# Cross attention in a decoder layer: the two halves of the output product in blocks (3, 0) and (3, 1) instead of (1, 6) and (1, 7)

## The reference

```python
def _L0_xattn_ref(x, context, context_mask, Wq, Wk, Wv, Wo):     # x is layer-normalised
    q = (x @ Wq).reshape(B, N, HEADS, hd).transpose(0, 2, 1, 3)   # 16 heads of 16
    k = (context @ Wk).reshape(B, M, HEADS, hd).transpose(0, 2, 1, 3)
    v = (context @ Wv).reshape(B, M, HEADS, hd).transpose(0, 2, 1, 3)
    scores = jnp.einsum('bhid,bhjd->bhij', q, k) * scale
    scores = jnp.where(context_mask[:, None, None, :], scores, max_neg)
    attn = jax.nn.softmax(scores, axis=-1)
    out = jnp.einsum('bhij,bhjd->bhid', attn, v)
    return out.transpose(0, 2, 1, 3).reshape(B, N, DIM) @ Wo      # x = x + this
```

## Time and profile before

| | |
|---|---|
| median of 3 runs | 1402.81 us (1402.61 to 1403.64) |
| the profiled execution | 1404.3 us |
| its span, first to last instruction | 1402.2 us |
| mean granted TensorE clock | 0.947 |
| PE busy | 1238.2 us, 88% of the span |
| DVE busy | 986.9 us, 70% |
| ACT busy | 629.1 us, 45% |
| POOL busy | 279.6 us, 20% |

### The profile page before, as it was taken

The page is one execution under the profiler, slowest core; times in us unless marked ns, Lnnn a source line. Parts: engine busy times, 40 slices in busy tenths (PEclk is TensorE's granted clock), DMA queues, the critical chain, the costliest instruction groups (busy, mean ns, idle before and its releaser), DMA issues. The chain is left out here.

```text
span 1402.2 us, 21352 instructions
## 1 busy us (share of the span) xinstructions
PE 1238.2 (88%) x6678; PEld 742.9 (53%) x6679; DVE 986.9 (70%) x1769; ACT 629.1 (45%) x1174; POOL 279.6 (20%) x224
## 2 busy tenths in 40 slices
PE   6699999999999996769999999899999724999976
PEld 4478777877787776413343343334333212666655
DVE  3787787778788773677778768666888166666646
ACT  4233333333333332217677757665877621433432
POOL 1322222222222221001200200120000023555540
PEclk9899999999999999759999999999999966999998
DMA  5000000000000000562810660173130070111125
GB/s 195 0 1 1 1 1 1 1 2 1 1 1 1 1 0 25 147 129 50 153 25 7 110 116 1 30 121 60 58 124 1 0 219 19 58 60 54 58 74 155
DMA packets 61367, 72.39 MB, mean 52 GB/s; under 512 B 14472, under 2 KB 52744, under 8 KB 60632
## 3 DMA queue, kind: packets, MB, share of 16 engines
q1 hardware_dynamic: 53064, 56.58, 17.3%
q0 software_dynamic: 3792, 10.36, 2.4%
q10 hardware_dynamic: 4416, 4.20, 0.9%
HBM read 52.08 MB, written 18.78 MB: 51 GB/s over the span
## 5 line engine op out<-in xcount | busy, mean ns | idle before, releaser
L1318 DVE TENSOR_REDUCE neg_max<-pS 128x1 f32<-128x1024 f32 x256 | 306.8, 1220 | 72.1 <-PE pS L1025 70.3
L1178 ACT ACTIVATE pt<-pR 128x512 f32<-128x512 f32 x512 | 287.4, 601 | 101.9 <-PE pR L1047 95.2
L1047 PE MATMUL pR<-qs,ks 100*128 100x512 bf16 (+1 forms) x512 | 188.6, 386 | 9.0 <-issue 4.2
L1025 PE MATMUL pS<-ks,qs 100*128 (+1 forms) x512 | 162.2, 401 | 11.2 <-DMA qs<-q_scr 5.7
L1059 PE MATMUL b_pO<-pt,b_v 128*32 128x512 f32 x1024 | 137.3, 608 | 3.3 <-ACT pt L1178 2.7
L1047 PEld LDWEIGHTS pR<-qs,ks 100*128 100x128 bf16 (+1 forms) x512 | 49.3, 98 | 155.2 <-issue 75.7
L232 PE MATMUL pP<-w_feat,a_xT 128*128 128x512 f32 x256 | 123.1, 606 | 2.7 <-DVE kf L488 1.5
L171 POOL TENSOR_TENSOR kf<-kf,fsum 128x2048 f32<-128x2048 f32 x16 | 57.9, 3620 | 215.6 <-DVE fsum L498 215.6
L171 POOL TENSOR_TENSOR qf<-qf,fsum 128x2048 f32<-128x2048 f32 x16 | 58.8, 3673 | 184.7 <-DVE fsum L498 184.7
L290 PE MATMUL pO<-v,am 128*128 128x96 f32 x512 | 91.2, 275 | 0.0
L406 ACT COPY qfT<-pT 128x512 f32<-128x512 f32 x64 | 37.0, 579 | 116.0 <-PE pT L258 116.0
(11 more groups left out here) (295 smaller groups left out, 2136.1 us busy)
## 6 DMA issues: line engine op xcount, KB each, us to landing
k_scr<-parts SPq DMA_DIRECT2D x24, 256.0 KB, 2.8
qs<-q_scr SPq DMA_DIRECT2D x18, 256.0 KB
ks<-k_scr SPq DMA_DIRECT2D x6, 768.0 KB
ks<-in_L_ffn_w_dram SPq DMA_DIRECT2D x2, 2048.0 KB, 9.9
ks<-in_L_ffn_w_dram SPq DMA_DIRECT2D x4, 1024.0 KB, 11.4
c_y<-y_rows SPq DMA_DIRECT2D x16, 256.0 KB, 3.2
cx<-in_ctx_dram SPq DMA_DIRECT2D x4, 768.0 KB, 9.6
q_scr<-parts SPq DMA_DIRECT2D x12, 256.0 KB, 2.6
```

Of the source, the lines that this page charges most:

```text
L1025: ins = pe.matmul(pS1[:, slot, 512 * half:512 * half + 512], qs[0:KR, bass.ds(par, 1), h, P * t:P * t + P].rearrange("r a n -> r (a n)"), ...
L1047: pe.matmul(ring[bank], ks[0:KR, bass.ds(par, 1), h, P * j:P * j + P].rearrange("r a n -> r (a n)"), qs[0:KR, bass.ds(par, 1), h, :].rearr ...
L1178: nc.scalar.activation(pt[:, j % 2, i, :], ring[bank], ACT.Exp).then_inc(exp_done, 1)
L1318: nc.vector.tensor_reduce(neg_max[:, hg % 2, u // G, u % G:u % G + 1], pS1[:, u % 2, :], AX_X, ALU.max, negate=True).then_inc(max_done, 1)
```

## The change

The plan has the steps ("y", 0) and ("y", 1) in blocks (3, 0) and (3, 1), where there was no step, instead of (1, 6) and (1, 7). By the order above, ("m_turn", 2) becomes the last and only step of (1, 6). The statistics of the last batch skip blocks (3, 0) and (3, 1), since those of batch 2's rows (the last four of the twelve) need its "y" steps done; they wait for the steps so far before the first and before the ninth tile.

```diff
-                (1, 6): [("m_turn", 2), ("y", 0)], (1, 7): [("y", 1)],
+                (1, 6): [("m_turn", 2)],
                 (2, 0): [("v", 0)], (2, 1): [("v", 1)], (2, 2): [("o_turn", 1)],
                 (2, 3): [("v", 2)], (2, 4): [("v", 3)], (2, 6): [("m_turn", 3)],
-                (3, 2): [("o_turn", 2)], (3, 6): [("m_turn", G)],
+                (3, 0): [("y", 0)], (3, 1): [("y", 1)], (3, 2): [("o_turn", 2)], (3, 6): [("m_turn", G)],
...
-                            if last and 2 <= hg and t_next < T - TB:
-
-                                if t_next == 0:
+                            if last and 2 <= hg and (hg, j) not in ((3, 0), (3, 1)) and t_next < T - TB:
+
+                                if t_next in (0, T - 2 * TB):
                                     wait(dve, emptied, start + n)
                                 nc.vector.bn_stats(stats[:, t_next, :], xr[:, t_next, :])
```

## The result

| | before | after |
|---|---|---|
| median of 6 runs | 1402.71 us (1400.61 to 1403.64) | 1394.34 us (1393.56 to 1397.29) |
| profiled execution, span | 1404.3, 1402.2 us | 1394.68, 1392.5 us |
| mean granted clock in it | 0.947 | 0.951 |

The ratio of the runs is 0.995, 95% interval 0.9937 to 0.9963: 7.0 us less, between 5.2 and 8.8. The two medians of the table differ by 8.4. The forecast was 1394.3 and 8.5 less. So the kernel is faster, by the two ratios a little less than forecast, though 8.5 lies inside both intervals. The median itself came out to the tenth, and part of that is luck, as the further profiles of the kernel before show.

What follows compares the result with a forecast made beforehand. PE was taken to bound cross attention. The terms -12.6 - 4.3 + 6.5 + 1.5 + 0.4 = -8.5 us took the median of 1402.8 to 1394.3 us, range 1391.6 to 1399.8.

Steps and rivals of the forecast that it cites:

- PE sets the pace, and a y step costs 1.73 us wherever it is full: Cross attention: y steps moved to (3,0) and (3,1) add 3.2 us per batch in batches 1 and 2, +6.5.
- The turn of the maxima becomes the last of its block, and batch 0 shows the plan: Batch 1: with the turn alone in (1,6), (1,6) and (1,7) take 7.50 us instead of 13.80, saving 6.3.
- The chain of DVE ends 0.7 us sooner than batch 0's: In (1,6), batch 1, DVE's split ends 2.31 us after the value group, 3.01 in batch 0; (1,6) takes 4.21.
- Batch 3 by its scores and ACT's pace: With y steps, (3,0) and (3,1) of batch 3 take 3.57 us each: +1.5, bounds 0.7 and 3.5.
- DVE's backlog in group 2 of batch 3, +0.4: DVE reaches group 2's statistics with the backlog of the split and the turn: +0.4 us, between 0 and 1.0.
- The low clock, 1.69 per batch in two batches: In (1,6), batches 1 and 2, the clock's fall under the y matmuls goes: 1.69 us per batch of the 6.3.
- Rival 1: The low clock was not there to win, or falls stay in some block: gain 5.1 us, 1397.7; chance 20%.
- Keys of the next batch: Needed at (2,6)'s first token unit, about 6 us sooner; their DMA falls quiet at 828.8, need about 840: covered.
- Rival 3, a stall at each turn of a batch: PE's 6.0 us stall between batches 1 and 2 also comes at the two other turns: +3.5, 1406.3; chance 4%.

Runs made afterwards that it cites:

- the two ratios: The changed kernel against the kernel before, measured twice, the second time with no edit: ratios 0.995 and 0.9952.
- One swap: The kernel before with the plan of (1,6) reordered, first y step ahead of the turn of group 2's maxima: 1395.06 us, ratio 0.9946.
- the changed kernel's repetition: The changed kernel run once more with no edit, beside the kernel before: 1396.14 us against 1402.50, ratio 0.9952.

## Why the prediction was right

- *PE sets the pace, and a y step costs 1.73 us wherever it is full.* Right: +6.47 of +6.5. Where the second step alone lies is worth 0.1 to 0.2 us in batches 1 and 2 at full clock.
- *The turn of the maxima becomes the last of its block, and batch 0 shows the plan.* Right: 7.57 against 7.50. The early turn alone cost 1.08 in batch 1 when put back.
- *The chain of DVE ends 0.7 us sooner than batch 0's.* Right: (1,6) is 4.32 in batches 1 and 2 and 4.92 in batch 0, 0.60 apart.
- *Batch 3 by its scores and ACT's pace.* +1.78 instead of +1.5: PE had no idle time left in (3,0) and (3,1) (3.70 of 3.70), and the worked 3.57 was 0.13 short per block. The measured sum lies within its bounds, 0.7 and 3.5.
- *DVE's backlog in group 2 of batch 3, +0.4.* Mis-sized, it measured 0.00: group 2 takes 23.37 us in both. DVE had caught up before the statistics began: it idles 0.40 us at 1054.01, waiting for PE, and the first statistic starts at 1055.15.
- *The low clock, 1.69 per batch in two batches.* The step that was off. The price was right (1.66); the count was not, as three of four profiles have the fall in one batch. I took the spread of three runs as evidence for both; it was none, since executions with one fall took 1401.2 to 1405.9 us. Rival 1 named this and had 20%; half of it is true. The ratio's -7.0 lies between the forecast and rival 1. That the median still fell on the forecast is luck.
- *Keys of the next batch.* Covered: no wait for them, and (2,6) and (2,7) of batch 1 take 7.04 against 7.03.
- *Rival 3, a stall at each turn of a batch.* It did not come: batch 0 to 1 takes 6.95 in both, and the last two blocks of batch 2 take 6.49 after 6.56.
- *What the prediction did not see:* that the move was not needed. The order within one block gives the same gain.

## What to carry to other kernels

In an engine's ordered queue, look for a step that needs the end of a short chain on another engine, and put independent work ahead of it, not directly behind it where that work needs the same read-out. One swap was worth as much here as moving the work to another group. When blocks repeat, cut the windows at an instruction that starts once in each and compare; a block of the same kernel that already lacks the step gave the estimate here (7.50 worked out, 7.57 measured). Before counting a low clock as a gain, profile the kernel a few more times.

## What the runs showed of the hardware

In batch 1 the clock fell under the first y matmuls in four of four executions of the kernel before, and in batch 2 in one of four, with equal waits of 1.4 and 1.1 us ahead of them in all. Two other kernels have these waits too: with the first y step back in (1,6) the clock fell in batch 1 and not in batch 2, with the turn early in batch 2 and not in batch 1. That makes 7 falls in 12 such blocks. In the six profiles without these waits it fell in none of the 12, 0.4 and 0.5 us being the longest left. Batch 0's block kept the full clock in the eleven profiles in which its longest wait was 1.1 us, and lost it in the one in which that was 2.1. A fall cost 1.5 to 1.7 us, read from batches 1 and 2 of one profile; the matmuls right behind the wait pay it. Single executions of the same program lie up to 4 us from the median (1398.4 to 1406.7 beside the changed kernel's repetition), and where the clock is low, in the stage before among others, is part of it.
